# A decoder layer on one core: the cross-attention mask written by a DMA, scratch rows of the stacks padded, one remainder moved by one half

## The chip, the cores and the metric

One core of a Trainium2 chip runs the whole program. The metric is the device time of one execution in microseconds, the median of three runs.

## What is computed

64 sequences of 128 tokens, width 128, go through self-attention, cross-attention over 77 context rows with a mask, and a feed-forward layer of 8 experts with the top 2 chosen per token. Each of the three adds to the residual stream. The part that the change touches is the cross-attention:

```python
q = _split_heads(query @ Wq.T + bq)      # 16 heads of 8
k = _split_heads(key @ Wk.T + bk)
scores = jnp.einsum('bhqd,bhkd->bhqk', q, k) / np.sqrt(D_K)
scores = jnp.where(mask[:, None, :, :] == 0, jnp.float32(-1000000000.0), scores)
p_attn = jax.nn.softmax(scores, axis=-1)
```

The mask is [64, 128, 77] and the same for all 16 heads.

## The kernel before

**Blocks and halves.** Four sequences (512 tokens) make a block; there are 16. The loop `steps` runs t from -3 to 17, and each engine runs its own copy of the body, ordered by semaphores. A turn of the loop has two halves of 16 units each. In the self half TensorE computes scores of self-attention twice: once with queries as rows, from which VectorE takes the maxima (`negm_m`, line 1099) for block t + 1, and once transposed and shifted by the maxima (line 1613), which ScalarE turns into `probs` (line 857) for block t. The cross half does the same for cross-attention: maxima (`negm_cm`) of block t - 1, probabilities of block t - 2. Between the units stand the smaller steps, each at a fixed unit number: projections, transposes, layer norms, the gate of block t - 3. `in_x` holds those of the self half, `in_y` those of the cross half.

**Stacks.** A head has only 8 numbers. To fill the rows of the matmul, each projection (`q`, `k` for self, `cq`, `ck` for cross) is split into three bf16 parts: the first by ScalarE from PSUM (`first`, lines 826 and 828), the remainder by VectorE (`remainder`, lines 1087 and 1089), the second part by ScalarE (`second`, line 839), the third by GpSimd (`third`, line 622). The first cross query part and the remainder read PSUM bank `wb[1]`, which the next user must wait for. SyncE then writes the parts to scratch in DRAM (`dump`, line 392) and reads them back in rows per head: `stack` (line 411) into `qkbig`, `stack_cross` (line 424) into `cbig`. One tensor takes six DMAs: runs of 24, 16 and 8 partitions, twice, once for each group of 8 heads. In DRAM the 8 heads of a row lie side by side, so a row of a `q`, `k` or `cq` stack is one piece of 8 KB, one of `ck` 4,928 bytes.

**Mask.** The cross score matmul has 77 rows more: on the key side the identity matrix (`places`), on the query side the mask as 0 or -2^100. GpSimd makes `mbT` [77, 512] from the mask of a block (line 741, last but one in its body, ahead of `third("cq", t)`). VectorE copies it to rows 0 to 76 of the query stack for all 16 heads in four copies of four heads (`masks`, line 1199) in the self half, at units 4, 5, 9 and 13.

**SyncE's order in a turn.** The cross stacks of block t - 1; the mask load `mk` of block t (line 441), which waits for `mbT` of block t - 1; the store of x3 (line 444); dumps of q, k (t + 2) and ck (t); the load of xin (line 455); the self stacks; the fold of the maxima into the self stack (line 432); loads of the context and of x again; the dump of cq (t). All of these go through one DMA queue, q1. ScalarE issues the fold of the cross maxima (line 835, three DMAs) on its own queue, q10, at unit 8 of the self half; ahead of the evacuation of the transposed x (line 819), which TensorE needs for the next projection.

**Who waits where.** The first matmul of a cross half (line 1602 on `cbig`) waits for the stacks cq and ck, for the mask, for the folded maxima, and for the last `negm_m`. The remainder of cq stands at unit 18 of the cross half, ahead of the first `negm_m` of the next self half, and ScalarE's second part of cq follows the cross half.

Of the kernel before, what the change touches and what calls it, by code (L numbers as in the profile page):

```python
# [23 lines left out]
BF16 = mybir.dt.bfloat16  # L24
# [7 lines left out]
SC = 77  # L32
# [20 lines left out]
MASKS = (4, 5, 9, 13)  # L53
# [48 lines left out]
def program(nc, x, ctx_in, mask, Wq, Wk, Wv, Wff, bff, xWq, xbq, xWk, xbk, xWv, xbv, xWo, xbo,  # L102
            Wp, WpT, sim, temp, W12, out):
    ctx = ExitStack()
    with ctx:
# [13 lines left out]
        def dram(name, shape, dt=F32):  # L119
# [9 lines left out]
        stk = {"q": dram("stk_q", [3, D, T], BF16), "k": dram("stk_k", [3, D, T], BF16),  # L129
               "cq": dram("stk_cq", [3, D, T], BF16), "ck": dram("stk_ck", [3, D, TC], BF16)}  # L130
# [126 lines left out]
        mb_ok, mask_ok = sem("mb_ok"), sem("mask_ok", len(MASKS))  # L257
# [123 lines left out]
        with nc.Block() as block:  # L381
            @block.sync
            def _(sp):
# [50 lines left out]
                def body(t, par):  # L434
                    if on_(t - 1):
                        for n, dst in (("ck", cks), ("cq", cqs)):
                            wait_block(sp, st_f["c"], t - 3)
                            stack_cross(n, t - 1, dst[1 - par])
                    if on_(t):
                        wait_block(sp, mb_ok, t - 1)  # L440
                        sp.dma_start(mk[:], mask_v[t]).then_inc(mk_in.sem, 16)
# [120 lines left out]
            def _(pool):  # L562
# [121 lines left out]
                def body(t, par):  # L684
# [52 lines left out]
                    if on_(t):  # L737
                        wait_block(pool, mask_ok, t - 1)
                        pool.wait_ge(mk_in.sem, mk_in.val(t))
                        pool.nop(nofuse=True)  # L740
                        nc.gpsimd.tensor_scalar(out=mbT[:].rearrange("k (s p) -> k s p", s=NS), in0=mk[:], scalar1=0.0,
                                                scalar2=MASKED, op0=ALU.is_equal, op1=ALU.mult).then_inc(mb_ok.sem, 1)
                        third("cq", t)
# [68 lines left out]
            def _(act):  # L812
# [56 lines left out]
                def body(t, par):  # L869
                    def in_x(u):  # L870
                        if 2 <= u < 2 + NS and on_(t + 2):
                            normalise("1", t + 2, xin, u - 2)
# [66 lines left out]
                    if on_(t):  # L939
                        second("cq", t)  # L940
# [116 lines left out]
            def _(dve):  # L1057
# [67 lines left out]

                def choose(b):
# [65 lines left out]
                def masks(b, dst, k):  # L1192

                    if k == 0:
                        dve.wait_ge(mb_ok.sem, mb_ok.val(b))
                        wait_block(dve, st_f["c"], b - 2)
                        dve.nop(nofuse=True)
                    n = H // len(MASKS)
                    nc.vector.tensor_copy(dst[0:SC, k * n:(k + 1) * n, :], mbT[:].unsqueeze(1).broadcast_to([SC, n, T]))\
                        .then_inc(mask_ok.sem, 1)  # L1200

                def body(t, par):
                    def in_x(u):
                        if u < NO and on_(t - 3):
                            divide("c", t - 3, u)
                        if u in MASKS and on_(t - 1):
                            masks(t - 1, cqs[1 - par], MASKS.index(u))
# [15 lines left out]
                    def in_y(u):  # L1223
# [18 lines left out]
                        if u == 18 and on_(t):  # L1242
                            wait_block(dve, part3["q"], t + 2)
                            remainder("cq", t, bq_c)
# [313 lines left out]
            def _(pe):  # L1558
# [115 lines left out]
                def body(t, par):  # L1674
# [84 lines left out]
                    if on_(t - 1):  # L1759
                        for n in ("cq", "ck"):  # L1760
                            pe.wait_ge(stacked[n].sem, stacked[n].val(t - 1))
                        if isinstance(t, int) and t - 1 < 2:
                            pe.wait_ge(ones_in.sem, ones_in.val(2 + t - 1))
                            pe.wait_ge(preset["ck"].sem, t)
                        pe.wait_ge(mask_ok.sem, mask_ok.val(t - 1))
                        maxi = ("cm", t - 1, cqs[1 - par], cks[1 - par], SC)
# [204 lines left out]
```

## Time and profile before

| | us |
|---|---|
| median of 3 runs | 1137.94 (1131.12 to 1140.22) |
| profiled execution, its time | 1140.97 |
| its span | 1139.2 |
| TensorE busy | 920.3 |
| VectorE busy | 803.7 |
| ScalarE busy | 795.4 |
| GpSimd busy | 623.9 |

The span is what the profiler recorded on the engines; the execution's own time is 1.8 us more. Busy time of TensorE has modelled ends. The turns of the loop with both attentions run from about 120 to 800 us; behind them stand the tiles of the experts. A turn in the middle takes about 42.6 us, half of it the self half.

### The profile page before, as it was taken

How to read it: one execution, taken by the hardware profiler on the slowest of the kernel's cores; microseconds unless marked ns; L12 is line 12 of the kernel's file. 1: busy time of each engine (PE TensorE's matmuls, PEld its weight loads, DVE VectorE, ACT ScalarE, POOL GpSimd, SP SyncE). 2: the span in 40 equal slices, each digit the busy share in tenths (PEclk: the TensorE clock that was granted, in tenths of full speed). 3: DMA queues.
4: the chain of work that ended last, by engine and by line, in shares of the span. 5: the costliest groups of instructions: out<-in, count | busy, mean ns of one | idle time of the engine just before them, and what ended most of it. 6: DMA issues, size and time to landing. Idle time of an engine off the chain costs nothing.

```text
span 1139.2 us, 30403 instructions
## 1 busy us (share of the span) xinstructions
PE 920.3 (81%) x11109; PEld 667.3 (59%) x11109; DVE 803.7 (71%) x2163; ACT 795.4 (70%) x1652; POOL 623.9 (55%) x823
## 2 busy tenths in 40 slices
PE   2447778888998998888998889877889999999900
PEld 1234546666666666656666656655666777787700
DVE  2743666787877877787877776474458888888816
ACT  2124547788778778777877767765778899999900
POOL 2423333466666676576576555555567556666650
PEclk9997779999999999999999989998899999999955
DMA  3245787766765766766766662661324666665329
GB/s 87 57 114 106 146 135 138 165 119 143 163 133 137 165 126 145 148 135 149 152 127 150 143 125 62 150 123 45 91 70 142 183 197 198 189 202 172 103 74 370
DMA packets 107564, 158.82 MB, mean 139 GB/s; under 512 B 16765, under 2 KB 81936, under 8 KB 102808
## 3 DMA queue, kind: packets, MB, share of 16 engines
q1 hardware_dynamic: 94536, 134.28, 51.7%
q0 software_dynamic: 9168, 17.21, 5.1%
q10 hardware_dynamic: 3712, 5.38, 1.3%
q8 instruction: 89, 1.46, 0.6%
q14 instruction: 59, 0.48, 0.2%
HBM read 103.12 MB, written 53.78 MB: 138 GB/s over the span
## 4 chain that ended last, share of the span: by engine, by line
PE 45%; DVE 18%; issue 10%; ACT 7%; POOL 7%; DMA 6%; SPq 5%; ACTq 1%; another core or an unknown queue 0%; POOLq 0%; DVEq 0%
PE pv L1627 6%; PE sc_m L1602 5%; PE wb L1585 4%; DVE negm_m L1099 4%; PE wb L1579 4%; PE wb L1574 4%; PE sc_a L1613 3%; PE pv L1856 2%; PE pv L1849 2%; PE pv L1850 2%; DVE on L1112 2%; DMA big<-y_d 2%; DVE negm_cm L1099 2%; POOL y_d L643 1%; DMA qkbig<-parts_m 1%
## 5 line engine op out<-in xcount | busy, mean ns | idle before, releaser
L857 ACT ACTIVATE probs<-sc_a 77x512 f32<-77x512 f32 (+1 forms) x512 | 301.7, 596 | 114.0 <-PE sc_a L1613 100.5
L643 POOL DMA_INDIRECT y_d<-yo,row x156 | 159.7, 1024 | 104.0 <-issue 41.2
L1099 DVE TENSOR_REDUCE negm_m<-sc_m 128x4 f32<-128x512 f32 x256 | 171.0, 683 | 57.8 <-PE sc_m L1602 52.1
L634 POOL DMA_INDIRECT xs_d<-xrow,slot_i x128 | 134.9, 1054 | 100.4 <-PE sc_a L1613 55.8
L1627 PE MATMUL pv<-probs,big 128*32 128x128 f32 x4096 | 172.0, 289 | 0.6 <-issue 0.6
L1099 DVE TENSOR_REDUCE negm_cm<-sc_m 128x4 f32<-128x308 f32 x256 | 116.5, 471 | 73.6 <-PE sc_m L1602 55.4
L1602 PE MATMUL sc_m<-qkbig 48*128 48x128 bf16 x1024 | 103.4, 234 | 51.8 <-DMA qkbig<-stk_k 17.0
L1307 DVE TENSOR_TENSOR gl<-g,gh 128x512 fp32r<-128x512 f32 x156 | 106.9, 687 | 41.3 <-ACT g L1002 24.5
L1602 PEld LDWEIGHTS sc_m<-qkbig 48*128 48x128 bf16 x1024 | 60.7, 100 | 121.0 <-issue 76.8
L1627 PEld LDWEIGHTS pv<-probs,big 128*32 128x32 f32 x4096 | 100.4, 112 | 37.8 <-issue 12.5
L1613 PE MATMUL sc_a<-qkbig 51*128 51x128 bf16 x1024 | 103.3, 229 | 8.6 <-ACT probs L857 8.5
L1613 PE MATMUL sc_a<-cbig 128*77 128x128 bf16 x1024 | 101.7, 224 | 3.9 <-issue 3.1
L1602 PE MATMUL sc_m<-cbig 125*128 125x77 bf16 x1024 | 80.1, 202 | 15.4 <-DVE negm_cm L1099 7.9
L1602 PEld LDWEIGHTS sc_m<-cbig 125*128 125x128 bf16 x1024 | 60.4, 100 | 33.2 <-DVE negm_cm L1099 18.3
L1613 PEld LDWEIGHTS sc_a<-cbig 128*77 128x77 bf16 x1024 | 70.1, 119 | 6.7 <-issue 4.2
L1856 PE MATMUL pv<-gl,vh 128*128 128x512 f32 x156 | 65.8, 422 | 4.4 <-DVE gl L1307 2.8
L1613 PEld LDWEIGHTS sc_a<-qkbig 51*128 51x128 bf16 x1024 | 60.2, 98 | 14.5 <-ACT probs L857 13.5
L1849 PE MATMUL pv<-gh,vh 128*128 128x512 f32 x156 | 63.3, 405 | 1.8 <-ACT gh L1002 1.0
L1002 ACT ACTIVATE gh<-sc_m,bias 128x512 fp32r<-128x512 f32 x78 | 54.4, 697 | 13.9 <-issue 13.5
L622 POOL TENSOR_TENSOR parts_q<-rest_q,parts_q 128x512 bf16<-128x512 f32 x16 | 20.0, 1247 | 77.7 <-ACT parts_q L839 77.7
L590 POOL TENSOR_SCALAR lnve<-lnmv 128x4 f32<-128x4 f32 x48 | 14.8, 309 | 85.1 <-DVE lnmv L1078 83.2
L1850 PE MATMUL pv<-gh,vl 128*128 128x512 f32 x156 | 61.4, 394 | 0.0
(214 smaller groups left out, 2326.2 us busy)
## 6 DMA issues: line engine op xcount, KB each, us to landing
wraw<-W_dram SPq DMA_DIRECT2D x39, 516.0 KB
xg<-xs_d SPq DMA_DIRECT2D x39, 260.0 KB
stk_q<-parts_q SPq DMA_DIRECT2D x16, 384.0 KB, 2.5
stk_k<-parts_k SPq DMA_DIRECT2D x16, 384.0 KB
qkbig<-stk_q SPq DMA_DIRECT2D x32, 192.0 KB
qkbig<-stk_k SPq DMA_DIRECT2D x32, 192.0 KB
stk_cq<-parts_cq SPq DMA_DIRECT2D x16, 384.0 KB, 2.7
cbig<-stk_cq SPq DMA_DIRECT2D x32, 192.0 KB
```

Source lines behind the costliest of these rows:

```text
L634: nc.gpsimd.indirect_dma_start(out=xs_d, in_=xrow[b % 2][:, c // 2, c % 2, :], in_offset=None, out_offset=bass.IndirectOffsetOnAxis(ap=slo ...
L643: nc.gpsimd.indirect_dma_start(out=y12_d, in_=yo[i % NY][:, c, :], in_offset=None, bounds_check=2 * B * S - 1, oob_is_err=False, out_offse ...
L857: nc.scalar.activation(probs[e % 4][0:rows], sc_a[e % 2][0:rows], ACT.Exp, scale=scale)\
L1002: nc.scalar.activation(part, h_banks[c], ACT.Gelu, bias=bias[i % NY][:, c:c + 1]).then_inc(g_ok.sem, 1)
L1099: nc.vector.tensor_reduce(out=negm[n][:, s, HG * g + 4 * half:HG * g + 4 * half + 4], in_=sc_m[u % 2][:, 0:4 * cols].rearrange("p (j k) -> ...
L1307: nc.vector.tensor_tensor(out=gl[c], in0=g[c], in1=hi32(gh[c]), op=ALU.subtract).then_inc(gl_ok.sem, 1)
L1602: i = nc.tensor.matmul(sc_m[u % 2][:, j * cols:(j + 1) * cols], qst[rows, slot + j, s * S:(s + 1) * S], kst[rows, slot + j, s * cols:(s + ...
L1613: i = nc.tensor.matmul(sc_a[u % 2][0:cols, j * S:(j + 1) * S], kst[rows, slot + j, s * cols:(s + 1) * cols], qst[rows, slot + j, s * S:(s ...
L1627: i = nc.tensor.matmul(pv[s // 2][VW * c:VW * (c + 1), slot * S:(slot + 1) * S], va[:, HG * s + 4 * half + c, g, :], probs[u % 4][:, c * S ...
L1849: nc.tensor.matmul(o, vh[par][:, w], gh[c], start=(c == 0), stop=False)
L1850: nc.tensor.matmul(o, vl[par][:, w], gh[c], start=False, stop=False)
L1856: nc.tensor.matmul(y_banks[par][:], vh[par][:, c * 128:(c + 1) * 128], gl[c], start=False, stop=(c == FC - 1)).then_inc(w2_done.sem, 1)
```

## The change

Three parts. The rows of the scratch tensors in DRAM are 32 elements longer than what is used, so that the 8 heads of a stack row no longer lie side by side: a stack row becomes 8 pieces of 1,024 bytes (616 for `ck`). The four VectorE copies of the mask go; instead SyncE issues one DMA per block, from `mbT` in SBUF to rows 0 to 76 of the query stack, the 16 heads at once, behind the cross stacks and ahead of the `mk` load. TensorE and GpSimd wait for that DMA (`mask_in`) where they waited for the copies (`mask_ok`). And the remainder of cq moves from unit 18 of the cross half to unit 0 of the next self half, behind its first `negm_m`; ScalarE's second part of cq moves to unit 1 of it, behind the first `probs`. The last block keeps the old places.

```diff
-MASKS = (4, 5, 9, 13)
+PAD = 32
...
-        stk = {"q": dram("stk_q", [3, D, T], BF16), "k": dram("stk_k", [3, D, T], BF16),
-               "cq": dram("stk_cq", [3, D, T], BF16), "ck": dram("stk_ck", [3, D, TC], BF16)}
+        stk = {n: dram(f"stk_{n}", [3, D, cols + PAD], BF16)[:, :, 0:cols]
+               for n, cols in (("q", T), ("k", T), ("cq", T), ("ck", TC))}
...
                         for n, dst in (("ck", cks), ("cq", cqs)):
                             wait_block(sp, st_f["c"], t - 3)
                             stack_cross(n, t - 1, dst[1 - par])
+                        sp.wait_ge(mb_ok.sem, mb_ok.val(t - 1))
+                        sp.dma_start(cqs[1 - par][0:SC, :, :], mbT[:].unsqueeze(1).broadcast_to([SC, H, T])).then_inc(mask_in.sem, 16)
                     if on_(t):
-                        wait_block(sp, mb_ok, t - 1)
                         sp.dma_start(mk[:], mask_v[t]).then_inc(mk_in.sem, 16)
...
-                        wait_block(pool, mask_ok, t - 1)
+                        wait_block(pool, mask_in, t - 1)
...
                     def in_x(u):
+                        if u == 1 and on_(t - 1) and t < NB:
+                            second("cq", t - 1)
...
-                    if on_(t):
+                    if t == NB - 1:
                         second("cq", t)
...
+                def last_queries(b):
+
+                    wait_block(dve, part3["q"], b + 2)
+                    remainder("cq", b, bq_c)
...
-                def masks(b, dst, k):
-
-                    if k == 0:
-                        dve.wait_ge(mb_ok.sem, mb_ok.val(b))
-                        wait_block(dve, st_f["c"], b - 2)
-                        dve.nop(nofuse=True)
-                    n = H // len(MASKS)
-                    nc.vector.tensor_copy(dst[0:SC, k * n:(k + 1) * n, :], mbT[:].unsqueeze(1).broadcast_to([SC, n, T]))\
-                        .then_inc(mask_ok.sem, 1)
-
                 def body(t, par):
                     def in_x(u):
+                        if u == 0 and on_(t - 1) and t < NB:
+                            last_queries(t - 1)
...
-                        if u in MASKS and on_(t - 1):
-                            masks(t - 1, cqs[1 - par], MASKS.index(u))
...
-                        if u == 18 and on_(t):
-                            wait_block(dve, part3["q"], t + 2)
-                            remainder("cq", t, bq_c)
+                        if u == 18 and t == NB - 1:
+                            last_queries(t)
...
-                        pe.wait_ge(mask_ok.sem, mask_ok.val(t - 1))
+                        pe.wait_ge(mask_in.sem, mask_in.val(t - 1))
```

VectorE at the seam from a cross half to a self half and up to the second mask copy, in a turn in the middle, before (`slot_i` ends the cross half, `negm_m` and `rden_c` are the self half's):

```order
L1190 CAST slot_i<-slot_f 128x8 [waits listed0,gate_step]
L1089 SCALAR_TENSOR_TENSOR rest_q<-wb,bq_c,parts_cq 128x512 [waits cq_part1,q_part3]
L1099 TENSOR_REDUCE negm_m<-sc_m 128x4 [waits m_sc_filled]
L1110 RECIPROCAL rden_c<-wb 128x32 [waits oTT_c_filled]
L1112 TENSOR_TENSOR on<-wb,rden_c 128x256 [waits rden_c_ok]
...
L1099 TENSOR_REDUCE negm_m<-sc_m 128x4 [waits m_sc_filled] x3
L1199 COPY cbig<-mbT 77x2048 [waits mb_ok,st_c_filled]
L1099 TENSOR_REDUCE negm_m<-sc_m 128x4 [waits m_sc_filled]
L1199 COPY cbig<-mbT 77x2048
```

The same place of the changed kernel:

```order
L1198 CAST slot_i<-slot_f 128x8 [waits listed0,gate_step]
L1102 TENSOR_REDUCE negm_m<-sc_m 128x4 [waits m_sc_filled]
L1092 SCALAR_TENSOR_TENSOR rest_q<-wb,bq_c,parts_cq 128x512 [waits cq_part1,q_part3]
L1113 RECIPROCAL rden_c<-wb 128x32 [waits oTT_c_filled]
L1115 TENSOR_TENSOR on<-wb,rden_c 128x256 [waits rden_c_ok]
...
L1102 TENSOR_REDUCE negm_m<-sc_m 128x4 [waits m_sc_filled] x5
L1125 TENSOR_TENSOR x<-wb,x2res 128x512 [waits x2res_ok,y_c_filled,x3_st]
```

The remainder of cq has moved behind one reduction, and the copies of the mask are gone; nothing else on VectorE changes its place.

SyncE's queue from the dump of cq to the dump of q, before (`stk_cq` is the scratch in DRAM, `cbig` the cross stacks):

```order
L392 DMA stk_cq<-parts_cq 128x3x512 [waits cq_part3]
L424 DMA cbig<-stk_ck 24x2464 [waits ck_dumped,st_c_filled]
L424 DMA cbig<-stk_ck 16x2464 x2
L424 DMA cbig<-stk_cq 24x4096 [waits cq_dumped,st_c_filled]
L424 DMA cbig<-stk_cq 8x4096 x2
L441 DMA mk<-mask_dram 77x4x128 [waits mb_ok]
L444 DMA x_d<-x 128x4x128 [waits y_c_drained]
L392 DMA stk_q<-parts_q 128x3x512 [waits q_part3]
```

And in the changed kernel:

```order
L392 DMA stk_cq<-parts_cq 128x3x512 [waits cq_part3]
L424 DMA cbig<-stk_ck 24x8x308 [waits ck_dumped,st_c_filled]
L424 DMA cbig<-stk_ck 16x8x308 x2
L424 DMA cbig<-stk_cq 24x8x512 [waits cq_dumped,st_c_filled]
L424 DMA cbig<-stk_cq 8x8x512 x2
L440 DMA cbig<-mbT 77x16x512 [waits mb_ok]
L442 DMA mk<-mask_dram 77x4x128
L445 DMA x_d<-x 128x4x128 [waits y_c_drained]
L392 DMA stk_q<-parts_q 128x3x512 [waits q_part3]
```

One DMA of 77 x 16 x 512 stands between the stacks and the mask load, and each stack row is in 8 pieces.

## Rows read from the trace of the kernel before

**Rows 1.** Page, part 1: busy us, share, instructions of each engine.

```profile
PE 920.3 (81%) x11109; PEld 667.3 (59%) x11109; DVE 803.7 (71%) x2163; ACT 795.4 (70%) x1652; POOL 623.9 (55%) x823
```

**Rows 2.** Windows of a cross half, then a self half; columns in the first row.

```profile
core 0: us, PE busy (x) PEld busy (x) DVE busy (x) ACT busy (x) POOL busy (x), PEclk, DMA share, GB/s
430.10:451.40 21.30, 19.96 (x324) 15.78 (x325) 14.73 (x64) 17.38 (x44) 13.59 (x22) 1.00 0.71 156
451.40:472.70 21.30, 17.77 (x295) 11.30 (x294) 18.92 (x37) 16.06 (x33) 14.27 (x20) 1.00 0.64 130
```

**Rows 3.** Tile mbT: the copies, ns min/median/max, first and last start.

```profile
L1199 DVE COPY cbig<-mbT x64: 655/681/1799, 121.6 to 758.4; 77x2048 bf16<-77x2048 bf16 x64
```

**Rows 4.** Timeline of VectorE: start, us, instruction, [idle before, releaser].

```profile
450.95 0.75 DVE L1089 SCALAR_TENSOR_TENSOR rest_q<-wb,bq_c,parts_cq 128x512 f32<-128x512 f32 x1 [1.08 <-ACT parts_cq L828]
451.62 0.68 DVE L1099 TENSOR_REDUCE negm_m<-sc_m 128x4 f32<-128x512 f32 x1
...
456.09 1.10 DVE L1199 COPY cbig<-mbT 77x2048 bf16<-77x2048 bf16 x1
457.43 0.69 DVE L1099 TENSOR_REDUCE negm_m<-sc_m 128x4 f32<-128x512 f32 x1 [0.23 <-PE sc_m L1602]
458.04 0.75 DVE L1199 COPY cbig<-mbT 77x2048 bf16<-77x2048 bf16 x1
...
463.22 0.68 DVE L1199 COPY cbig<-mbT 77x2048 bf16<-77x2048 bf16 x1
...
466.37 0.69 DVE L1099 TENSOR_REDUCE negm_m<-sc_m 128x4 f32<-128x512 f32 x1 [1.87 <-PE sc_m L1602]
...
469.27 1.68 DVE L1199 COPY cbig<-mbT 77x2048 bf16<-77x2048 bf16 x1
...
472.07 0.67 DVE L1099 TENSOR_REDUCE negm_m<-sc_m 128x4 f32<-128x512 f32 x1
```

**Rows 5.** Timeline of TensorE in the same self half.

```profile
453.68 0.23 PE L1602 MATMUL sc_m<-qkbig 48*128 48x128 bf16 x1 [0.91 <-DVE negm_m L1099]
...
464.91 1.10 PE L1579 MATMUL wb<-xnT,w_q 128*128 128x512 f32 x2 [1.16 <-ACT xnT L819]
...
471.35 1.18 PE L1627 MATMUL pv<-probs,big 128*32 128x128 f32 x32
472.81 0.32 PE L1602 MATMUL sc_m<-cbig 125*128 125x77 bf16 x4 [0.27 <-DVE negm_m L1099]
```

**Rows 6.** Timeline of ScalarE: second part of cq, the fold's issues in two turns.

```profile
451.74 0.63 ACT L839 ACTIVATE parts_cq<-rest_q 128x512 bf16<-128x512 f32 x1 [0.40 <-DVE rest_q L1089]
...
461.26 2.85 ACTq L835 DMA_DIRECT2D cbig<-parts_m  x3
...
504.66 1.81 ACTq L835 DMA_DIRECT2D cbig<-parts_m  x3
```

**Rows 7.** Timeline of GpSimd: third part of cq.

```profile
452.45 1.15 POOL L622 TENSOR_TENSOR parts_cq<-rest_q,parts_cq 128x512 bf16<-128x512 f32 x1 [0.52 <-ACT parts_cq L839]
```

**Rows 8.** Timeline of SyncE's DMA issues.

```profile
453.63 0.38 SPq L392 DMA_DIRECT2D stk_cq<-parts_cq  x1
...
456.64 2.25 SPq L424 DMA_DIRECT2D cbig<-stk_cq  x6
...
470.43 0.38 SPq L392 DMA_DIRECT2D stk_q<-parts_q  x1
...
475.94 2.29 SPq L411 DMA_DIRECT2D qkbig<-stk_q  x6
```

**Rows 9.** DMA queues, 457 to 461 us: packets, MB, share of 16 engines.

```profile
q1 hardware_dynamic: 123, 0.45, 79.7%
```

**Rows 10.** The same, 466 to 469.5 us.

```profile
q1 hardware_dynamic: 582, 0.28, 35.4%
```

**Rows 11.** The same, 471 to 473 us (one dump of q).

```profile
q1 hardware_dynamic: 400, 0.39, 55.7%
```

**Rows 12.** Windows: a stretch between two groups of transfers.

```profile
469.40:471.00 1.60, 1.22 (x32) 0.74 (x31) 1.60 (x2) 1.60 (x5) 1.44 (x2) 1.00 0.00 0
```

**Rows 13.** Page, part 6: dump of cq, KB, us from issue to landing.

```profile
stk_cq<-parts_cq SPq DMA_DIRECT2D x16, 384.0 KB, 2.7
```

More of the change, by code:

```diff
@@ L256, in program @@
         x_in, c_in, mk_in = sem("x_in", 16), sem("c_in", 16), sem("mk_in", 16)
-        mb_ok, mask_ok = sem("mb_ok"), sem("mask_ok", len(MASKS))
+        mb_ok, mask_in = sem("mb_ok"), sem("mask_in", 16)
         xres_ok, x2res_ok = sem("xres_ok"), sem("x2res_ok")
```

## The prediction

> **What bounds the kernel now.** I read the page first, then one turn in the middle. VectorE is busy 71% of the span [rows 1], but a mean over stages says little, so I cut the turn into its halves. In the cross half TensorE is busy 19.96 of 21.30 us and VectorE 14.73; in the self half it is the other way, VectorE 18.92 and TensorE 17.77 [rows 2]. The four mask copies stand in the self half, in the engine that is fullest there. The question is which wait ends last, and that is read from the timelines. TensorE stands still in this self half at few places: 0.91 us for a `negm_m` at 453.68, 1.16 us for ScalarE's transposed x at 464.91, and 0.27 us for the last `negm_m` ahead of the first cross matmul at 472.81 [rows 5]. VectorE itself waits for TensorE right behind the first copy (0.23 us) and for 1.87 us shortly behind the third [rows 4]. So three of the four copies fill time in which VectorE would wait anyhow. The third resource is the DMA queue. It has nothing to move between 469.4 and 471.0 [rows 12], so all that the cross half needs has landed some 3 us before 472.81. That is the slack that the change uses.
>
> **Part 1, the copies go.** In this turn they take 1.10 + 0.75 + 0.68 + 1.68 = 4.21 us [rows 4]; over the run 64 copies with a median of 0.68 [rows 3]. The first three are covered: TensorE isn't ready behind the first, and the third is followed by the wait of 1.87 us. The fourth ends at 470.95, two reductions and a remainder follow, and the last reduction ends at 472.74. TensorE's `pv` is through at 471.35 + 1.18 = 472.53, so without that copy 0.27 us go, and the end of `pv` is late next. If VectorE's chain mattered everywhere, the 0.91 us would go as well; if it matters nowhere, nothing goes. I take 0.27, since the 0.91 stands ahead of all copies.
>
> **Part 2, the remainder moves.** Now VectorE waits 1.08 us for ScalarE's first part of cq, runs the remainder (0.75), then the first `negm_m` at 451.62 [rows 4]. After, the reduction goes first and fills part of that wait, then the remainder, then the division as before. The second reduction comes about 0.1 us earlier, so I count 0.1 us. The end of the remainder goes from 451.70 to about 452.3, and with it the second part of cq (451.74 now [rows 6]), the third (452.45 [rows 7]) and the dump on SyncE's queue (453.63 [rows 8]): 0.6 us later. Behind that dump stand the cross stacks, and since this change the mask. The bank `wb[1]` is free 0.6 us later too; the transpose that waits for it has the 0.91 us behind it as cover, and costs up to 0.6 us if that cover is gone. Parts 1 and 2 together give 0.37 us per block, 0.37 x 16 = 6 us, as long as nothing else arrives later.
>
> **Part 3, the mask as a DMA.** It moves 77 x 16 pieces of 1 KB, 1,232 packets, 1.26 MB, from SBUF to SBUF on queue q1, right behind the stacks. No row shows such a transfer, so I bound it from both sides. Fast end: a dump of 384 packets of 1 KB takes 55.7% of 16 engines for 2.0 us, that is 17.8 engine-us or 46 ns a packet [rows 11]; 1,232 x 46 ns / 16 = 3.5 us. Slow end: in the stretch in which the stacks run, q1 moves 0.45 MB in 4 us, 0.112 MB/us, with 79.7% of the engines' time taken [rows 9]; 1.26 / 0.112 = 11.2 us. The stacks write 8 to 24 partitions, the dump reads 128, the mask writes 77; it has the dump's packets, but not its spread. No row is clearly nearer, so I take the middle, 7.3 us.
>
> When does it start? From 466 us on q1 moves 582 packets with 0.28 MB, 480 bytes each [rows 10]: the pieces of 8 KB are over, and the small loads and stores behind them run. With the dump 0.6 us later the stacks are through at 466.6. The mask is through at 466.6 + 7.3 = 473.9. A dump lands 2.7 us after its issue [rows 13], and its packets take 17.8 / 16 = 1.1 us of that; of the remaining 1.6 us I put 0.3 behind the last packet. The first cross matmul stands at 472.81 [rows 5]. So TensorE waits for the mask, and the cross half begins near 474.2, 1.4 us later than now. The 0.37 us of the first parts are lost in this wait. What is queued behind the mask DMA on SyncE's queue: the mask load, the store of x3, then the dump of q at 470.43, whose landing the self stack at 475.94 waits for [rows 8]. The 820 small packets behind the mask cost 0.354 x 16 x 3.5 / 582 = 34 ns each [rows 10], 1.7 us on 16 engines, and end at 475.6; the dump of q lands near 475.6 + 1.1 + 0.3 = 477.0; the self stack would be issued at 477.3 in a turn that is 1.4 us longer. That just fits, so I add nothing. The wait recurs in each of 16 blocks: 16 x 1.4 = 22.4 us.
>
> The Trainium skill (DMA: Bandwidth & Descriptors, "Why a DMA increments its semaphore by 16 and not by 1") says that a DMA runs on the largest number of engines up to 16 that divides the slowest dimension of both sides. For 77 partitions that is 11 engines of 112 packets each. With the 46 ns of the rows it gives an estimate of 5.2 us, so 472.1 with the semaphore, just in time, which is the first rival below; no row here shows the split.
>
> **The padding.** Bytes stay the same, and pieces of 8 KB become 8 of 1 KB. In rows 9 a KB of the stacks costs 51.0 engine-us / 0.45 MB = 0.113 us, against 0.046 for the dump's packets [rows 11]. Is it the length of the piece or where it goes? If it is the length, the 1.23 MB of the two cross stacks gain up to half of their time, some 5 us; if packets have a cost of their own, they lose up to 1 us. I take zero: the engines that write one stack still write the same few partitions. SyncE's issue time doesn't grow with the pieces: the dump with 384 takes 0.38 us, six stacks with 8 to 24 pieces each take 2.25 [rows 8].
>
> The Trainium skill (SBUF — State Buffer, "Door 1: The DMA port swizzle") says that DMA bandwidth depends on how many of 16 SBUF ports the partitions reach, and that four neighbouring partitions share one. A run of 8 partitions would then be slow whatever the size of its pieces, which speaks against a gain by the padding. The low rate in rows 9 agrees with it, but the rate alone doesn't tell it from a cost of long pieces.
>
> **Sum.** 1140.97 + 22.4 = 1163.4 for the profiled execution. That one lies 3.0 us above the median of the runs, so 1160 for the median.
>
> **Rivals.** *The mask lands in time.* Either the stacks get shorter in pieces of 1 KB, or the mask runs near the dump's rate (up to 5.5 us would do). For it: 46 ns a packet in rows 11. Against: rows 9, in which a KB costs two and a half times as much. Then only the 0.37 us per block show: 1137.9 - 6 = 1132.
>
> *VectorE's relief shows.* With the mask in time and the self half paced by VectorE (18.92 of 21.30 busy [rows 2]), the 0.91 and 0.27 us of TensorE's waits for `negm_m` [rows 5] go together: 1.18 x 16 = 19 us, 1119. This is the case on the other side; it decides if the mask lands before 472 and the wait at 453.68 falls with the reordered remainder. Against: the 0.91 us stand ahead of the copies, and the waits behind them are TensorE's and ScalarE's.
>
> *ScalarE's fold is held up.* Its three DMA issues take 2.85 us in one turn and 1.81 in the next [rows 6], so 1 us of ScalarE's time depends on something outside it. They stand at 461.26, while now the queue will hold the mask's 1,232 packets, and TensorE waits for the `xnT` behind them already (1.16 us). If the issue lasts 3.5 us longer, the self half ends 3.5 us later, more than the 1.4 us of the mask: 16 x 3.5 = 56, 1194. Against: SyncE's and ScalarE's issues show no such growth elsewhere.
>
> **Chances.** My forecast 0.46, mask in time 0.24, relief shows 0.18, fold held up 0.12. A measurement of this kernel can tell about 1% (11 us) from no change. Of the forecast's case a little (0.06) lies within 1%, if the mask takes under 6.6 us. So faster 0.18, same 0.30, slower 0.52. For the range: at 3.5 us the mask is free (1132), at 11.2 us it costs 5.3 us a block (1223). I leave out the far end of that and a part of the relief: 1122 to 1194.
>
> **What would show it.** Right: in the self half VectorE is about 4 us less busy, TensorE's first cross matmul waits some 1 to 2 us for a DMA into `cbig`, the turn is 44 us, and the DMA engines are busy up to that matmul. The windows of the DMA queue show whether the stacks keep 0.113 us a KB. Wrong: the wait at the start of the cross half is for `negm_m` or `pv` as now, or the idle times in the self half lie behind `xnT` and the fold.

## The result, and the profile after

The changed kernel takes 1256.13 us (median of 4 runs, 1247.25 to 1261.07), the kernel before 1139.08 on the same chip (4 runs, 1131.12 to 1143.67). The ratio is 1.102, 95% interval 1.096 to 1.108: 117 us slower. The forecast of 1160 had the direction, but the time lies 62 us above the upper end of its range.

The page of the changed kernel, parts 1, 3, 4 and 6:

```profile
PE 942.4 (75%) x11109; PEld 693.7 (55%) x11109; DVE 754.9 (60%) x2099; ACT 793.1 (63%) x1652; POOL 605.6 (48%) x823
...
q1 hardware_dynamic: 157432, 154.47, 57.2%
...
DMA cbig<-mbT 22%; SPq L424 6%; PE sc_m L1599 3%; PE sc_a L1610 3%; PE pv L1624 3%; POOL mbT L742 2%; POOL xs_d L635 2%; PE wb L1659 2%; PE pv L1846 2%; PE pv L1853 2%; PE pv L1847 2%; PE wb L1571 2%; POOL lnrs L594 2%; DMA big<-y_d 2%; PE wb L1582 2%
...
cbig<-mbT SPq DMA_DIRECT2D x16, 1232.0 KB
stk_q<-parts_q SPq DMA_DIRECT2D x16, 384.0 KB, 8.7
```

VectorE has indeed lost 48.8 us of work against [rows 1], and it bought nothing. The mask's DMA alone makes 22% of the chain that ended last. A dump of q, which was 2.5 us in flight before, is now 8.7. The waits of TensorE say how much of the 117 us stands at one place:

```profile
PE sc_m L1599 <- DMA cbig<-mbT: 99.0, 16, 13.3
PE sc_m L1599 <- DMA qkbig<-parts_m: 17.7, 2, 11.6
```

All 16 blocks wait for the mask, 6.2 us each in the mean, 13.3 at the longest. The second row isn't new: the kernel before waits 14.5 us in the same two places. Next, one turn in the middle, cut by windows into the self half up to its last matmul, the wait, and the cross half:

```profile
core 0: us, PE busy (x) PEld busy (x) DVE busy (x) ACT busy (x) POOL busy (x), PEclk, DMA share, GB/s
476.90:499.13 22.23, 18.97 (x306) 12.14 (x302) 15.77 (x33) 16.72 (x34) 15.76 (x23) 1.00 0.71 126
499.13:504.76 5.63, 0.00 (x1) 0.03 (x1) 0.00 (x0) 0.97 (x2) 0.54 (x3) 0.64 0.93 265
504.76:526.30 21.54, 19.95 (x314) 16.35 (x314) 14.39 (x62) 15.86 (x41) 10.65 (x16) 0.94 0.79 145
```

The same edges in the kernel before, the cross half ahead of the self half:

```profile
430.16:450.47 20.31, 19.03 (x314) 15.12 (x315) 14.28 (x62) 16.45 (x43) 12.60 (x22) 1.00 0.73 160
450.47:472.81 22.34, 18.70 (x307) 11.97 (x303) 19.42 (x37) 17.04 (x35) 15.31 (x20) 1.00 0.62 127
```

These edges are the first matmul of the cross half and the first of the self half in TensorE's timeline (the next cross half begins at 472.81 [rows 5]):

```profile
430.16 0.31 PE L1602 MATMUL sc_m<-cbig 125*128 125x77 bf16 x4 [0.27 <-DVE negm_m L1099]
...
450.47 0.39 PE L1602 MATMUL sc_m<-qkbig 48*128 48x128 bf16 x4
```

So before, the self half was 472.81 - 450.47 = 22.34 us and the cross half 20.31, 42.65 in all. Now it is 22.23 + 5.63 + 21.54 = 49.40. In that turn 5.52 us come between the halves and 1.23 within the cross half. A third number stands in the window of the wait: the DMA engines are 93% busy, while TensorE does nothing and the other compute engines next to nothing.

SyncE's issues and TensorE's matmuls around the wait, from the timelines:

```profile
480.69 0.38 SPq L392 DMA_DIRECT2D stk_cq<-parts_cq  x1
481.17 2.64 SPq L424 DMA_DIRECT2D cbig<-stk_ck  x6
483.90 2.34 SPq L424 DMA_DIRECT2D cbig<-stk_cq  x6
486.29 0.91 SPq L440 DMA_DIRECT2D cbig<-mbT  x1
487.24 7.96 SPq L442 DMA_DIRECT2D mk<-mask_dram  x1
495.25 3.08 SPq L445 DMA_DIRECT2D x_d<-x  x1
498.37 2.00 SPq L392 DMA_DIRECT2D stk_q<-parts_q  x1
```

```profile
478.74 0.66 PE L1659 MATMUL wb<-ident,oT 128*128 128x128 f32 x4 [0.52 <-DVE rest_q L1092]
...
480.06 0.23 PE L1599 MATMUL sc_m<-qkbig 48*128 48x128 bf16 x1 [0.33 <-DVE negm_m L1102]
...
504.76 0.42 PE L1599 MATMUL sc_m<-cbig 125*128 125x77 bf16 x4 [5.63 <-DMA cbig<-mbT]
504.98 1.10 PE L1659 MATMUL wb<-ident,oT 128*128 128x128 f32 x4
...
509.08 0.31 PE L1599 MATMUL sc_m<-cbig 125*128 125x77 bf16 x4
```

From the issue of the dump of cq to the first cross matmul it is 504.76 - 480.69 = 24.07 us; before it was 472.81 - 453.63 = 19.18, and the stacks were not even the last thing in it. The first matmuls behind the standstill run long: four transposes take 1.10 us at 504.98 and 0.66 at 478.74. The clock that TensorE was granted, the third number from the right, tells why:

```profile
499.13:500.00 0.87, 0.00 (x1) 0.00 (x0) 0.00 (x0) 0.83 (x2) 0.54 (x3) 1.00 1.00 274
501.00:504.76 3.76, 0.00 (x0) 0.03 (x1) 0.00 (x0) 0.00 (x0) 0.00 (x0) 0.50 0.96 282
504.76:507.00 2.24, 2.24 (x19) 2.18 (x20) 1.33 (x4) 0.20 (x1) 0.00 (x0) 0.50 0.95 263
508.00:510.00 2.00, 1.73 (x36) 1.43 (x32) 1.68 (x5) 1.98 (x5) 1.01 (x1) 1.00 0.85 155
```

It was at its upper level (1.00, 2.4 GHz) when the standstill began, at its lower one (0.50, 1.2 GHz) from 501 us on and through the first matmuls of the cross half, and at the upper one again from 508 us.

The turn in the middle is not the dearest. The first turn of the changed kernel, SyncE's queue, and the matmul that waits longest of all:

```profile
122.45 0.39 SPq L392 DMA_DIRECT2D stk_cq<-parts_cq  x1
122.88 2.49 SPq L536 DMA_DIRECT2D xs_d<-xrow  x2
125.42 1.67 SPq L397 DMA_DIRECT2D cbig<-ones  x2
127.13 2.53 SPq L424 DMA_DIRECT2D cbig<-stk_ck  x6
129.70 2.54 SPq L424 DMA_DIRECT2D cbig<-stk_cq  x6
132.28 0.92 SPq L440 DMA_DIRECT2D cbig<-mbT  x1
133.25 10.85 SPq L442 DMA_DIRECT2D mk<-mask_dram  x1
...
151.87 0.42 PE L1599 MATMUL sc_m<-cbig 125*128 125x77 bf16 x4 [13.32 <-DMA cbig<-mbT]
```

Here stores of 2 x 260 KB of empty rows stand between dump and stacks. They do so for blocks 0, 1 and 2 alone (six stores in the trace, 117.4 to 202.1 us of the kernel before), and with them the step from dump to cross half is 29.4, 30.2 and 27.1 us, against 21.9 to 24.1 in the other 13 blocks. Counted from first matmul to first matmul, the first three self halves (the first of them reaches back to 41 us, over turns that have no cross half yet) have become longer by 13.5, 11.7 and 9.6 us, the other eleven by 4.9 us in the mean, and the 13 whole cross halves by 1.7 us in the mean.

### The profile page after: what moved, and what is told of

The parts are those of the page before. It is cut to its first block, busy times and chain, and to the rows that moved or that the text cites. A ratio compares the mean times of both kernels' runs of the same rounds, so it can differ in the third digit from the quotient of the medians.

```text
span 1259.3 us, 30339 instructions
## 1 busy us (share of the span) xinstructions
PE 942.4 (75%) x11109; PEld 693.7 (55%) x11109; DVE 754.9 (60%) x2099; ACT 793.1 (63%) x1652; POOL 605.6 (48%) x823
## 3 DMA queue, kind: packets, MB, share of 16 engines
q1 hardware_dynamic: 157432, 154.47, 57.2%
## 4 chain that ended last, share of the span: by engine, by line
PE 32%; DMA 26%; issue 12%; POOL 11%; SPq 11%; DVE 5%; ACT 2%; POOLq 0%; DVEq 0%; ACTq 0%
DMA cbig<-mbT 22%; SPq L424 6%; PE sc_m L1599 3%; PE sc_a L1610 3%; PE pv L1624 3%; POOL mbT L742 2%; POOL xs_d L635 2%; PE wb L1659 2%; PE pv L1846 2%; PE pv L1853 2%; PE pv L1847 2%; PE wb L1571 2%; POOL lnrs L594 2%; DMA big<-y_d 2%; PE wb L1582 2%
## 5 line engine op out<-in xcount | busy, mean ns | idle before, releaser
L644 POOL DMA_INDIRECT y_d<-yo,row x156 | 159.7, 1024 | 106.8 <-issue 42.9
L1599 PE MATMUL sc_m<-cbig 125*128 125x77 bf16 x1024 | 87.7, 215 | 108.1 <-DMA cbig<-mbT 99.0
L1599 PE MATMUL sc_m<-qkbig 48*128 48x128 bf16 x1024 | 102.5, 232 | 49.9 <-DMA qkbig<-parts_m 17.7
L1599 PEld LDWEIGHTS sc_m<-cbig 125*128 125x128 bf16 x1024 | 69.2, 109 | 124.9 <-issue 106.0
L1610 PE MATMUL sc_a<-cbig 128*77 128x128 bf16 x1024 | 110.4, 237 | 1.7 <-ACT probs L858 1.1
L1610 PEld LDWEIGHTS sc_a<-cbig 128*77 128x77 bf16 x1024 | 77.3, 129 | 4.6 <-ACT probs L858 3.6
L591 POOL TENSOR_SCALAR lnve<-lnmv 128x4 f32<-128x4 f32 x48 | 12.0, 251 | 119.5 <-DVE lnmv L1081 117.6
L1659 PE MATMUL wb<-ident,oT 128*128 128x128 f32 x256 | 54.1, 351 | 9.8 <-DVE rest_q L1092 6.2
```

The source lines that it names most:

```text
L644: nc.gpsimd.indirect_dma_start(out=y12_d, in_=yo[i % NY][:, c, :], in_offset=None, bounds_check=2 * B * S - 1, oob_is_err=False, out_offse ...
L1599: i = nc.tensor.matmul(sc_m[u % 2][:, j * cols:(j + 1) * cols], qst[rows, slot + j, s * S:(s + 1) * S], kst[rows, slot + j, s * cols:(s + ...
L1610: i = nc.tensor.matmul(sc_a[u % 2][0:cols, j * S:(j + 1) * S], kst[rows, slot + j, s * cols:(s + 1) * cols], qst[rows, slot + j, s * S:(s ...
L1659: i = nc.tensor.transpose(wb[bank][:, slot * S:(slot + 1) * S], oT[n][:, k, slot * S:(slot + 1) * S], ident[:])
```

## The experiments

They ask three things: which part of the change costs how much, what limits the mask's DMA, and why the two parts that the prediction put at nothing cost something. Medians of the kernel before differ between sessions, so each result is a ratio to the kernel before on the same chip, with its 95% interval in brackets. A trace is a single execution, and those of two kernels often come from different chips: a difference of a few us between two whole traces says nothing.

### Which part

**e1: the change without the padding.**

```
-PAD = 32
+PAD = 0
```

> The changed kernel with unpadded scratch rows, so a stack row is one piece of 8 KB again; the mask still goes by DMA. Theory 'pieces': stacks in pieces of 1 KB run longer than in pieces of 8 KB, and what they lose is handed on to the mask behind them. The stacks end 2 to 3 us earlier after the dump of cq than in the changed kernel, and the time falls by 16 x 2.5 = 40 us, to about 1215. Rival 'mask': the whole wait is the mask's own movement; then the time stays at 1250 to 1260.

1218.4 us, ratio 1.089 (1.083 to 1.095). TensorE's wait for the mask falls from 99.0 to 77.6 us:

```profile
PE sc_m L1599 <- DMA cbig<-mbT: 77.6, 16, 10.9
```

Pieces of 1 KB make nothing shorter; without them the kernel is quicker by 1.3% of the time before. Theory "pieces" had the sign and not the size: it asked for 40 us, 3.5%. That its 1215 us stand near 1218.4 is the chip, on which the kernel before takes 1120.83. Over blocks 3 to 13 the stacks land 14.7 us behind the dump of cq, against 15.5 in the changed kernel: 0.8 us earlier and not 2 to 3.

**e2: the padding alone, in the kernel before.**

```
-  stk = {"q": dram("stk_q", [3, D, T], BF16), ...}
+  stk = {n: dram(f"stk_{n}", [3, D, cols + 32], BF16)[:, :, 0:cols] ...}
```

> The kernel before with padded scratch rows alone; the mask is copied by VectorE as before. Theory 'pieces': the cross stacks end 2 to 3 us later, inside their slack of 3 us, but the self stacks and the fold have less slack, so 0 to 2 us a block show: 1139 to 1170. Rival 'mask': nothing changes, 1139 within 5 us.

1132.62 us, ratio 1.0127 (1.007 to 1.018). The padding costs 1.3% with and without the mask's DMA (the second number is a difference of two ratios, good to about 0.8 points). The page of the changed kernel has 157,432 packets on q1, that of e1 this row, for the same bytes:

```profile
q1 hardware_dynamic: 114424, 154.47, 53.5%
```

57.2% of 1259.3 us is 720.3 us, 53.5% of 1216.7 is 650.9: 43,008 more packets take 16 x 69.4 = 1,110 engine-us more, some 26 ns a packet. This price isn't fixed: the pages of e6 and e12, which differ by the padding and the move, give 56.5% of 1201.3 us and 55.2% of 1176.5, that is 11 ns.

**e3: no copies and no mask DMA at all.** In the kernel before the mask rows are set to zero once; the mask per block is left out.

```
+  for i in range(2):
+      nc.vector.memset(cqs[i][0:SC, :, :], 0.0).then_inc(mask_ok.sem, 1)
...
-  if u in MASKS and on_(t - 1):
-      masks(t - 1, cqs[1 - par], MASKS.index(u))
```

> The kernel before without the four mask copies: the mask rows of both query stacks are set to 0 once at the start and not written again (so the mask of a block is left out). It shows what the copies cost. My prediction counted 0.27 us a block: 4 us, 1135. Rival 'relief': VectorE paces the self half and 1.2 us a block or more go: 1120 or less.

1128.76 us, ratio 1.007 (1.004 to 1.010). The two memsets stand ahead of everything, on VectorE:

```profile
6.32 3.47 DVE L1067 MEMSET cbig<- 77x4096 uint32 x1 [0.78 <-issue]
10.59 3.47 DVE L1067 MEMSET cbig<- 77x4096 uint32 x1 [0.80 <-issue]
```

The first dump of q is issued 8.2 us later than in the kernel before, 27.95 against 19.79; 8.2 us are 0.7% of the time. If all of that delay reaches the end, what is left is 1.000, within 0.35% either way. It may not: in the traces the first self matmul is 8.5 us later, the first cross matmul 3.2 and the fourteenth cross half 5.6. Then the kernel without copies is the slower one. Either way all 64 copies together are worth at most 0.35%, 4 us, which is just what the prediction gave them. The rival "VectorE's relief shows" falls with this, and with it the reason to move the mask at all.

**e8: the remainder's move alone**, in the kernel before.

```
+  if u == 0 and on_(t - 1) and t < NB:
+      last_queries(t - 1)
...
-  if u == 18 and on_(t):
-      wait_block(dve, part3["q"], t + 2)
-      remainder("cq", t, bq_c)
```

> The kernel before with only the remainder of cq and its second part moved into the next self half; scratch rows unpadded, mask by four VectorE copies. My prediction counted 0.1 us a block, 2 us less: ratio 0.998. Rival 'later dump': the dump of cq comes 0.6 us later and delays the cross stacks, which land in their slack, so nothing shows, 1.000; more than 1.003 would mean that the later bank or dump is waited for.

1151.07 us, ratio 1.013 (1.008 to 1.018). The surprise of the study: the part that was to gain 0.1 us a block costs 15 us. Two waits of TensorE in its trace aren't there before:

```profile
PE wb L1671 <- DVE rest_q L1092: 6.2, 12, 0.5
...
PE sc_m L1611 <- DMA cbig<-stk_cq: 4.1, 1, 4.1
```

The first is in 12 blocks, the second in the first turn; a wait of 4.4 us for which the trace names no releaser follows in the second. The waits for `negm_m` fell at the same time, from 17.7 to 12.6 us. So the move was cut in two.

**e9 and e10: the move for blocks 3 to 14 alone, and for blocks 0 to 2 alone.**

```
+  def moved(b): return b >= 3 and b < NB - 1     # e10: b < 3
-  if u == 0 and on_(t - 1) and t < NB:
+  if u == 0 and on_(t - 1) and moved(t - 1):
```

> The kernel before with the remainder's move alone, and that only for blocks 3 to 14; blocks 0 to 2 are done as before, no padding, the four mask copies stay. Theory 'early': the move costs something only where the dump of cq is followed by the extra stores of empty rows into xs_d and the loads of ones (blocks 0 to 2, landings of the cross stacks 20 us behind the dump instead of 14), since only there does TensorE wait for the stacks; then this kernel runs as the one before, ratio 1.000 (0.996 to 1.004). Theory 'every block': the later remainder holds up the transposes into wb[1] in each self half, 0.9 us a block; then 12 of 15 moved blocks cost 1.010.

> The other part of it: the move for blocks 0 to 2 alone. Theory 'early': nearly all of the 1.013 of the full move, 1.008 to 1.013, with a wait of some 4 us for cbig<-stk_cq or the like in the first turns. Theory 'every block': 3 of 15, 1.002 to 1.003.

e9 has 1.0052 (1.001 to 1.009), e10 1.0079 (1.004 to 1.012); together the 1.013 of e8. Neither theory is right alone. The 12 late blocks cost 5.9 us (1.5 to 10 by the interval), 0.5 each, and their trace has the wait for the bank:

```profile
PE wb L1676 <- DVE rest_q L1097: 5.7, 11, 0.5
```

The sizes match, but this wait doesn't explain the cost, because the one for `negm_m` right behind it has become shorter. The stretch that holds both, from the first matmul of the self half to the transposes of `on`, takes 3.96 us in the mean of 11 turns of e9, 3.76 in the kernel before and 3.87 in e10, where these blocks are unchanged: 0.1 to 0.2 us a block. From the fourth self half to the fourteenth cross half (240 to 686 us of the kernel before) TensorE is idle for 41.1 us before and for 40.9 in e9. Where the rest of the 5.9 us lies stays open.

The three early ones cost 8.9 us (5 to 13 by the interval). In their trace TensorE stands twice at the start of a cross half:

```profile
136.98 0.42 PE L1616 MATMUL sc_m<-cbig 125*128 125x77 bf16 x4 [4.42 <-DMA cbig<-stk_cq]
...
179.71 0.42 PE L1616 MATMUL sc_m<-cbig 125*128 125x77 bf16 x4 [4.46 <-issue]
...
244.65 0.39 PE L1616 MATMUL sc_m<-qkbig 48*128 48x128 bf16 x4
```

The kernel before has these at the same matmuls:

```profile
178.81 0.30 PE L1602 MATMUL sc_m<-cbig 125*128 125x77 bf16 x4 [1.37 <-DMA cbig<-parts_m]
...
239.71 0.39 PE L1602 MATMUL sc_m<-qkbig 48*128 48x128 bf16 x4
```

Its cross half of block 0 begins at 137.28 without a wait, so the first wait of e10 only takes up a lead. From there to the end of the third cross half e10 takes 107.67 us and the kernel before 102.43: 5.2 us more, 1.2 of them up to the end of the second wait and 4.0 behind it, where the granted clock was 0.93 (179.71 to 223.00 us) and 1.00 before. As wholes these two executions took 1138.09 and 1140.97 us, so they show where the three early blocks lose time, and don't prove how much. The early blocks are dear because the extra stores leave the cross stacks no slack: from the dump of cq to the first cross matmul it is 20.3 us for block 0 and 21.6 for block 1 in the kernel before, with the stacks landing 0.7 and 0.6 us ahead of that matmul, and 16.4 to 19.6 from block 2 on, with the stacks 1.0 us ahead in block 2 and 2.2 to 5.7 in the others. Why a dump 0.6 us later makes waits longer than 0.6 stays open.

**e11: the mask's DMA alone**, without padding and with the remainder where it was.

```
-PAD = 32
+PAD = 0
...
-  if u == 0 and on_(t - 1) and t < NB:
-      last_queries(t - 1)
...
-  if u == 18 and t == NB - 1:
+  if u == 18 and on_(t):
```

> The mask's DMA alone: the changed kernel without the padding and with the remainder of cq where it was. Theory 'sum': padding, move and mask each delay the same landing, so their costs add, 1.102 - 0.013 - 0.013 = 1.076, and TensorE's waits for cbig<-mbT fall to some 60 us in all. Theory 'slack': the cross half has the 1 to 3 us of slack that the prediction read from the trace, and the mask alone lands 1.8 us behind the old start, 16 x 1.8 = 29 us and some 15 us in the first turns: 1.035 to 1.045.

1204.01 us, ratio 1.064 (1.058 to 1.070), between the two theories. TensorE's wait for the mask is what "sum" asked for, the time isn't:

```profile
PE sc_m L1595 <- DMA cbig<-mbT: 59.2, 16, 8.1
```

Alone, the three parts cost 6.4% + 1.3% + 1.3% = 9.0%; on top of one another 6.4%, then 2.5% for the move (e1 against e11), then 1.3% for the padding, 10.2%. The move costs twice as much once the mask is what TensorE waits for. The later dump then goes through in every block and not only in the first three. In the means of blocks 3 to 13 the dump of e1 stands 3.78 us behind the start of the self half, that of e11 3.02; the mask lands 21.6 and 21.5 us behind the dump; so TensorE waits 3.77 us instead of 2.85, and the cross half behind the wait takes 0.7 us more. That is 1.6 of the 1.8 us that 2.5% are for each of 16 blocks.

### What limits the mask's DMA

**e4: the mask in two DMAs, rows 0 to 63 and 64 to 76.**

```
+  for lo, hi in ((0, 64), (64, SC)):
+      sp.dma_start(cqs[1 - par][lo:hi, :, :], mbT[lo:hi]....broadcast_to([hi - lo, H, T]))
```

> The changed kernel with the mask DMA cut into rows 0 to 63 and rows 64 to 76. Theory 'engines': one DMA of 77 partitions loads a part of the 16 engines (11, if it is split evenly) with 112 packets each; cut in two it is at most 80 each, the mask takes 0.71 of its time, some 3 us a block less, 1210. Rival: the partitions or the shared reading of one tile limit it; then 1250 to 1260.

1243.22 us, ratio 1.110 (1.104 to 1.116). No gain: the mask lands 7.6 us behind the stacks in the mean of blocks 3 to 13, against 7.1 in the changed kernel. So the number of engines on the mask isn't what bounds it.

**e5: the mask read from DRAM** instead of `mbT`, after one store of it.

```
-  sp.dma_start(cqs[1 - par][0:SC, :, :], mbT[:]....)
+  sp.dma_start(cqs[1 - par][0:SC, :, :], mask_d[1 - par]....)
...
+  sp.dma_start(mask_d[par], mbT[:]).then_inc(mask_out.sem, 16)
```

> The changed kernel, but the mask of a block is first stored to a scratch tensor in DRAM (77 KB, ahead of the dump of cq) and the DMA of 16 heads reads it from there. Partitions written, packets and their size are the same; only the side that is read has moved out of SBUF. Theory 'read and write share': reading each row 16 times from the same partitions that are written is what makes the mask take 7 to 8 us behind the stacks; from DRAM it takes about 5, and 2.5 to 3 us a block go, ratio to the kernel before 1.06. Rival 'written side or queue': the same time as the changed kernel, ratio 1.10.

1256.73 us, ratio 1.103 (1.096 to 1.110), as the changed kernel itself. The wait only changes its name:

```profile
PE sc_m L1603 <- DMA cbig<-mask_d: 100.2, 16, 12.2
```

Reading 16 times from the same rows of SBUF isn't the limit.

**e6: the mask ahead of the dump of cq** in SyncE's queue.

```
+  sp.wait_ge(mb_ok.sem, mb_ok.val(t))
+  wait_block(sp, st_f["c"], t - 2)
+  sp.dma_start(cqs[par][0:SC, :, :], mbT[:]....)
   dump("cq", t)
```

> The changed kernel with the mask DMA issued ahead of the dump of cq, as soon as the mask of the block is made, instead of behind the cross stacks. The same bytes on the same queue, but the 2 to 3 us in which the DMA engines have nothing to do there are used. Theory 'queue': what counts is when the queue has worked off stacks and mask together; 2.5 us a block earlier, 40 us, ratio 1.065. Rival 'order': what counts is only that the mask stands last; then the wait goes as a whole, ratio 1.02 or less.

1203.45 us, ratio 1.061 (1.054 to 1.067), as "queue" asked. The same bytes by the same engines cost 4 points less where they run while the third part of cq is still being made. The wait is for the stacks now:

```profile
PE sc_m L1601 <- DMA cbig<-stk_cq: 41.6, 13, 5.8
```

**e7: eight heads by DMA, eight by two copies on VectorE.**

```
+MASKS = (4, 5)
...
-  sp.dma_start(cqs[1 - par][0:SC, :, :], mbT[:]....broadcast_to([SC, H, T]))
+  sp.dma_start(cqs[1 - par][0:SC, 8:H, :], mbT[:]....broadcast_to([SC, H - 8, T]))
```

> The changed kernel with heads 8 to 15 of the mask by DMA and heads 0 to 7 by two VectorE copies at units 4 and 5. Theory 'queue': the mask takes 4.1 us instead of 8.3 behind the stacks, the wait of 5.6 falls to 1.4 and most of the clock's loss with it: 5 us a block less, ratio 1.03. Rival 'fixed cost of the wait': the ratio falls by half or less, 1.05 or more.

1196.22 us, ratio 1.053 (1.046 to 1.061), the rival's number and not that of "queue". The wait is no fixed cost, though: it falls to 1.6 us in the mean of blocks 3 to 13, from 5.1, as "queue" said. What stays is padding and move. If they count as in e2 and e8, they are 2.6 of the 5.3 points, so half the mask costs 2.7 and the whole 7.6; by e1 and e11 the move's share is larger. The first half is cheaper, as it should be where the cross stacks have some slack.

**e12: the mask ahead, without padding and move.** e6 and e11 in one.

> The mask's DMA issued ahead of the dump of cq, without the padding and with the remainder where it was: the mildest form of the mask by DMA. Theory 'sum': from e6_mask_ahead (1.0605) the padding (0.013) and the move (0.025, from e1_no_pad 1.089 against e11_mask_only 1.064) go, so 1.02 to 1.035. Theory 'saturated': with the mask ahead the cross stacks behind it are late by what the mask takes in the queue in any case, and dump and mask overlap, so the move no longer counts: only the padding's 0.013 goes, 1.045 to 1.05. In neither case is it faster than the kernel before.

1180.94 us, ratio 1.045 (1.040 to 1.051): "saturated". Against e6 only the padding's share goes. The mildest form of the mask by DMA found here costs 50 us more than the copies. In its trace one stretch holds nearly nothing but the mask and the dump (474 to 481 us, the DMA queues):

```profile
q1 hardware_dynamic: 1382, 1.42, 73.8%
```

0.738 x 16 x 7 / 1382 = 60 ns for a packet of 1 KB, those of the mask and of the dump together, where the prediction took 46 from the dump [rows 11]. No variant beat the kernel before, and e3 says that sparing the copies can win 0.35% at most. The better kernel is the one before.

## Why the prediction was wrong

**The copies, 0.27 us a block.** The self half without the wait has gone from 22.34 to 22.23 us: 0.1. VectorE's relief is real (19.42 to 15.77 us between the same edges) and doesn't show in the time; for the whole kernel e3 puts it at 0.35% or less. The reading that the copies fill waits was right.

**The move, a gain of 0.1 us and a dump 0.6 us later.** The delay was right for this turn: the dump is issued 480.69 - 476.90 = 3.79 us behind the start of the self half, before 453.63 - 450.47 = 3.16 (2.85 in the mean of 11 turns). The gain was wrong in its sign: with 0.33 us left for `negm_m` and 0.52 for `rest_q` in its place, the stretch takes 0.1 to 0.2 us more in the mean (e9); in this turn it's 3.97 us, before 4.03. The fear for `wb[1]` was not the cost: the 0.91 us of cover did pay for nearly all of it. What was missed is the first three blocks, where the stacks land less than 1.1 us ahead of the cross half and the move costs 8.9 us (e10), and that behind a late mask each later dump is a longer wait: 2.5% between e11 and e1.

**The mask, 1.4 us a block.** The prediction had dump to cross matmul at 474.2 - 454.2 = 20.0 us: 12.4 up to the end of the stacks, 7.3 for the mask, 0.3 to the landing. The mask alone (e11), in the turn that lies in the same place, has

```profile
444.00 0.38 SPq L392 DMA_DIRECT2D stk_cq<-parts_cq  x1
...
466.73 0.36 PE L1595 MATMUL sc_m<-cbig 125*128 125x77 bf16 x4 [4.00 <-DMA cbig<-mbT]
```

that is 22.73, and the changed kernel 24.07. The trace records when a DMA updates its semaphore. By the last update of each, in us:

| | stacks landed behind the dump | mask landed behind the stacks | first matmul behind the mask |
|---|---|---|---|
| prediction | 12.4 | 7.3 | 0.3 |
| kernel before, this turn | 14.15 | | |
| e11, this turn | 14.59 | 8.00 | 0.14 |
| changed kernel, this turn | 15.64 | 8.30 | 0.13 |
| kernel before, mean of blocks 3 to 13 | 14.2 | | |
| e11, mean | 14.6 | 6.9 | 0.2 |
| e1, mean | 14.7 | 6.9 | 0.2 |
| changed kernel, mean | 15.5 | 7.1 | 0.2 |

The step that failed is "the stacks are through at 466.6". That moment was read from the last large packet, and the stacks of the kernel before land at 467.78, 14.15 us behind their dump: 1.8 us of the mask's wait were there to be seen. The landing of a dump was a bad measure for that of six stacks. The second step is the padding, put at zero: it makes the stacks land 0.8 us later and the mask 0.3 us later still (changed kernel against e1). The mask's own 7.3 us were about right, and that is luck, since they were only the middle between 3.5 and 11.2.

Why the mask takes 7 to 8 us and not less, no run isolates; I offer a reading. Between 496.3 and 504.7 us, from the end of the stacks to the release, the queue moved

```profile
q1 hardware_dynamic: 2428, 2.00, 83.4%
```

of which the mask is at most 1,232 packets and 1.26 MB. The rest is the mask load `mk`, issued right behind the mask, and the store of x3 and the dumps of q, k and ck, issued at 495.25 and later. The engines worked on these before the mask's last packet had landed (the first updates of x3 come at 500.02, those of the dump of q at 502.45, the mask's last at 504.63); the prediction let everything behind the mask wait its turn. In the quiet stretch of e12 73.8% of 16 engines are at work, which is near 11 of 16. The Trainium skill (DMA: Bandwidth & Descriptors, "Why a DMA increments its semaphore by 16 and not by 1") gives 11 engines for 77 partitions, each of which reports once; the trace agrees, with 11 late updates of the mask's semaphore per block. But the time worked out from it, 5.2 us, was too low, and e4, made for more engines, brought nothing.

**The padding, zero.** It costs 1.3%, in e2 and between e1 and the changed kernel. Of the two theories the prediction weighed, that of packets with a cost of their own was right, and its "up to 1 us" fits the 0.8 us by which the cross stacks land later. From the rule of the Trainium skill (SBUF — State Buffer, "Door 1: The DMA port swizzle") that DMA bandwidth depends on how many ports the partitions reach, the prediction argued against a gain by shorter pieces. No gain came; no run here changes the ports.

**1.4 us times 16.** The multiplication failed twice. The first three self halves got 35 us longer, of 110 us in all the halves; one turn of the middle, where the stacks of the kernel before land 5.0 us ahead of the cross half, doesn't stand for them. And the cross half was taken as fixed. Behind a standstill TensorE's granted clock is lower, 0.64 in the window of the wait and 0.94 in the cross half behind it, where both halves had 1.00 before [rows 2]. By the matmul of the same place, 509.08 and 433.51, the cross half has lost 0.97 of its 1.23 us, and most of that stretch ran at 0.50. The wait is paid for, and then some of the work behind it again. So the mask alone, forecast at 22.4 us, costs 6.4%, 72 us: TensorE waits 59.2 us for it, 2.85 a block in the middle, 6.7 to 8.1 in the first three.

**The rivals.** "Mask lands in time" was wrong by 5.6 us. "ScalarE's fold is held up" was wrong: three issues took 1.81 us in this turn, the smaller of the two times in [rows 6], and all 16 folds together 32.0 us, before 30.9. The queue's back pressure did come, but at SyncE: 7.96 us for the small load behind the mask, where it took 0.31 in e8. It held up only transfers that nobody waited for; in the self halves of the middle TensorE doesn't wait for `qkbig`.

```profile
487.64 1.81 ACTq L836 DMA_DIRECT2D cbig<-parts_m  x3
```

## What to carry to other kernels

Before work is moved off an engine, take it out altogether and time that: if the kernel is hardly faster with the work gone, as in e3, no way of doing it elsewhere can gain more than that run leaves, and a DMA behind transfers that another engine needs can lose much. Read the slack of a queue in the first turns as well as in the middle, and from the landing of the transfer, not from its last packets. When a new wait appears in a list, see which wait has gone in its place before it is given a price: the 0.52 us for the bank came with 0.4 to 0.6 us less for `negm_m`, and of the 5.7 us that seemed to explain a cost, 1 to 2.4 were real.

## What the runs showed that was not expected

- Back pressure shows at the issuing engine behind one large DMA: the next issue on SyncE took 7.96 us behind the mask, 10.85 in the first turn, the one after it 3.08, and the dump of q 2.00 instead of 0.38. In e6 and e12, where the dump follows the mask, 7.5 and 7.8 us fall on the six stacks of ck, which take 2.4 otherwise.
- Cutting 8 KB pieces into 1 KB pieces costs 11 to 26 ns for each packet more, though the partitions written stay the same.
- A packet of 1 KB of mask and dump took about 60 ns where little else ran, and reading the mask from DRAM instead of SBUF changed nothing (1.103 against 1.102).
